# The root of the mean square in a decoder kernel: multiplied in by GpSimd behind the gating, from a product in four 32-column tiles

## The reference

```python
gg = (x @ Wg.T).reshape(B, L, H, DH)
o = o * jax.lax.rsqrt(jnp.mean(o * o, -1, keepdims=True) + EPS)
o = o * o_norm_w * jax.nn.silu(gg)
return (o.reshape(B, L, KEY_DIM) @ Wo.T, final_state)
```

## Time and profile before

| | |
|---|---|
| median of 3 timed runs | 1228.74 us (1227.93 to 1232.73) |
| profiled execution, its own time | 1221.33 us |
| its span | 1219.5 us |
| TensorE busy | 1145.7 us, 94% |
| TensorE weight loads | 790.1 us, 65% |
| VectorE busy | 814.1 us, 67% |
| ScalarE busy | 716.0 us, 59% |
| GpSimd busy | 499.3 us, 41% |

### The profile page before, as it was taken

One profiled execution on the slowest core, in us unless ns is written; L12 is line 12 of the kernel. 1 busy time (PEld: TensorE's weight loads), 2 busy tenths in 40 slices (PEclk: granted clock), 3 DMA queues, 4 the chain that ended last, 5 costly groups with the idle time before them and its releaser, 6 DMA issues.

```text
span 1219.5 us, 30002 instructions
## 1 busy us (share of the span) xinstructions
PE 1145.7 (94%) x12192; PEld 790.1 (65%) x12192; DVE 814.1 (67%) x1454; ACT 716.0 (59%) x1212; POOL 499.3 (41%) x709
## 2 busy tenths in 40 slices
PE   7888899999999999999998989859999999999987
PEld 2444455555555555555555556649998998998976
DVE  4897667768768768668576665665665566655552
ACT  3776467677677676776775866624444434445433
POOL 1659576575675774773774811100011000001000
PEclk9999799999999999999998999989999999999999
DMA  3123222323323223243326422161111122111100
GB/s 118 46 52 79 66 52 60 107 58 72 87 58 93 68 73 77 77 128 89 91 73 150 151 62 72 47 235 45 44 45 49 50 52 70 44 44 48 30 17 10
DMA packets 134602, 88.07 MB, mean 72 GB/s; under 512 B 79264, under 2 KB 118048, under 8 KB 133568
## 3 DMA queue, kind: packets, MB, share of 16 engines
q1 hardware_dynamic: 133312, 85.93, 25.9%
q10 hardware_dynamic: 1152, 0.21, 0.1%
HBM read 54.77 MB, written 14.55 MB: 57 GB/s over the span
## 4 chain that ended last, share of the span: by engine, by line
PE 75%; POOL 8%; DVE 5%; issue 4%; ACT 3%; SPq 2%; DMA 2%; ACTq 0%; POOLq 0%; DVEq 0%
PE proj L467 20%; PE out L1494 5%; PE turned_v_chain L1494 5%; PE gram L482 4%; PE turned_v_chain L1560 4%; PE proj L1552 4%; PE proj L1433 4%; POOL inverse L1204 3%; POOL rank_one L1201 3%; PE out L491 2%; PE turned_v_chain L596 2%; PE gram L1468 2%; PE decays L497 2%; PE turned_v_chain L629 2%; DVE conv L992 2%
## 5 line engine op out<-in xcount | busy, mean ns | idle before, releaser
L992 DVE SCALAR_TENSOR_TENSOR conv<-proj,kq_weights,conv 128x504 f32<-128x504 f32 (+2 forms) x261 | 189.9, 731 | 24.4 <-ACT conv L736 17.7
L467 PE MATMUL proj<-xT,vg_weights 128*128 128x512 f32 x384 | 190.6, 620 | 1.8 <-DVE conv L992 1.6
L1791 POOL TENSOR_TENSOR rope<-rope_part,rope_part 128x512 f32<-128x512 f32 x32 | 40.0, 1271 | 364.8 <-DVE rope_part L1730 364.8
L992 DVE SCALAR_TENSOR_TENSOR conv<-proj,vg_weights,conv 128x504 f32<-128x504 f32 (+2 forms) x192 | 140.8, 734 | 44.9 <-ACT conv L736 40.0
L467 PE MATMUL proj<-xT,kq_weights 128*128 128x512 f32 x348 | 164.5, 599 | 0.2 <-DVE conv L992 0.2
L1204 POOL TENSOR_TENSOR inverse<-inverse,rank_one 128x30 f32<-128x30 f32 (+14 forms) x240 | 125.2, 522 | 18.8
L1201 POOL TENSOR_TENSOR rank_one<-inverse 128x30 f32<-128x30 f32 (+14 forms) x240 | 117.7, 490 | 15.9
L467 PEld LDWEIGHTS proj<-xT,vg_weights 128*128 128x128 f32 x384 | 68.4, 192 | 65.6 <-issue 59.8
L467 PEld LDWEIGHTS proj<-xT,kq_weights 128*128 128x128 f32 x348 | 62.4, 190 | 72.8 <-issue 70.3
L1569 ACT ACTIVATE rstd<-rstd 128x1 f32<-128x1 f32 x48 | 9.8, 203 | 142.6 <-DVE rstd L1677 142.6
L482 PEld LDWEIGHTS gram<-keys_q 128*64 128x64 f32 x896 | 57.6, 138 | 54.7 <-ACT keys_q L747 36.4
(11 more groups left out here) (244 smaller groups left out, 2464.0 us busy)
## 6 DMA issues: line engine op xcount, KB each, us to landing
kq_weights<-in_kq_w SPq DMA_DIRECT2D x32, 390.0 KB, 3.5
vg_weights<-in_vg_w SPq DMA_DIRECT2D x32, 390.0 KB, 4.0
o_scratch<-oT SPq DMA_DIRECT2D x32, 256.0 KB, 2.9
o_in<-o_scratch SPq DMA_DIRECT2D x16, 512.0 KB, 4.1
diagonal<-gram_decayed SPq DMA_DIRECT2D x128, 32.0 KB, 1.9
inverse<-inverse SPq DMA_DIRECT2D x32, 128.0 KB, 2.7
q_first<-rope SPq DMA_DIRECT2D x128, 32.0 KB, 1.9
q_second<-rope SPq DMA_DIRECT2D x128, 32.0 KB, 1.9
```

The source lines that it names most:

```text
L467: mm = e.matmul(bank(c, u)[:], w[:, (k * 3 + c % 3) * 128:(k * 3 + c % 3 + 1) * 128], xT[g][:, k, :], start=(k == 0), stop=(k == KD - 1))
L992: e.scalar_tensor_tensor(acc(c, u)[:, :, back:], src[:, :, 0:S - back], weights(c, u)[:, j:j + 1], acc(c, u)[:, :, back:], ALU.mult, ALU.a ...
L1791: e.tensor_tensor(turned[half][:].rearrange("p b r q -> p r b q"), parts[2 * half][:], parts[2 * half + 1][:], op).then_inc(s_turned, 1)
```

## The change

Units 0 to 21 (`by_rows`) get a new path; units 22 to 31, whose norm falls into the drain, keep the 128x128 product and the full 128x512 Ln and Exp.

- The product: four matmuls with 32 of the 128 columns of `ones_mean`, one for each 128 tokens; matmul j writes the 32 partitions from 32j on, columns 0 to 127 of VB. So partition 32j holds the means of the j-th quarter of the tokens.
- Ln and Exp work on 128x128 (`rs4`).
- SyncE, at the head of its slot, issues four DMAs that spread row 32j of `rs4` to all 128 partitions of the j-th quarter of `o_rs`. The stores of the KRS kind move from the end of their slot to behind these, in the next slot.
- For all units VectorE now gates with silu(G) alone and waits for neither Ln nor Exp; it does so as soon as OB and the gate are there. GpSimd multiplies `oT` by `o_rs` in place, behind the first part of its elimination (`s_gr`), in the drain too, where VectorE's `scale_gate` goes. SyncE's store waits for that.

```diff
+        by_rows = lambda u: u < U - LAG - 1
@@ sync
                 for s in range(SLOTS):
+                    if live(uo) and by_rows(uo):
+                        e.wait_ge(s_rs, uo + 1)
+                        wait(e, s_gr, uo)
+                        for j in range(4):
+                            e.dma_start(o_rs[:, j * TILE:(j + 1) * TILE],
+                                        rs4[RB * j:RB * j + 1, None, :].broadcast_to([1, 128, TILE])).then_inc(d_rs, 16)
+                    rotated = prepare_at(s - 1)
+                    if rotated is not None and rotated[1] == KRS:
+                        prepare_store(*rotated)
...
                     if live(uo):
-                        e.wait_ge(s_og, uo + 1)
+                        e.wait_ge(s_gr, uo + 1)
                         e.dma_start(o_scratch[:, 4 * group(uo):4 * group(uo) + 4, head(uo), :],
...
-                    if now is not None:
+                    if now is not None and now[1] != KRS:
                         prepare_store(*now)
@@ tensor
                 def norm(u):
                     e.wait_ge(s_osum, u + 1)
-                    e.matmul(VB, ones_mean[:], o_sum[:], start=True, stop=True).then_inc(s_norm, 1)
+                    if by_rows(u):
+                        for j in range(4):
+                            mm = e.matmul(VB[rows(j), 0:TILE], ones_mean[:, 0:RB], o_sum[:, j * TILE:(j + 1) * TILE],
+                                          start=True, stop=True)
+                    else:
+                        mm = e.matmul(VB, ones_mean[:], o_sum[:], start=True, stop=True)
+                    mm.then_inc(s_norm, 1)
@@ scalar
                 def silu_gate(u):
-                    wait(e, s_gr, u - 2)
+                    wait(e, s_og, u - 2)
...
-                        wait(e, s_og, uo)
-                        e.activation(o_rs[:], VB, ACT.Ln, scale=float(2 ** O_SHIFT), bias=guard[:, 0:1]).then_inc(s_ln, 1)
+                        if by_rows(uo):
+                            wait(e, d_rs, 64 * uo)
+                            o_ln, o_mean = rs4[:], VB[:, 0:TILE]
+                        else:
+                            e.wait_ge(s_gr, uo)
+                            o_ln, o_mean = o_rs[:], VB
+                        e.activation(o_ln, o_mean, ACT.Ln, scale=float(2 ** O_SHIFT), bias=guard[:, 0:1]).then_inc(s_ln, 1)
...
-                        e.activation(o_rs[:], o_rs[:], ACT.Exp, scale=-0.5).then_inc(s_rs, 1)
+                        e.activation(o_ln, o_ln, ACT.Exp, scale=-0.5).then_inc(s_rs, 1)
@@ vector
-                def scale_gate(u):
-                    e.wait_ge(s_rs, u + 1)
-                    e.wait_ge(s_silu[G], u + 1)
-                    wait(e, s_og, u)
-                    e.tensor_tensor(o_rs[:], flat(gate[u % 3]), o_rs[:], ALU.mult).then_inc(s_gr, 1)
...
                     def gate_output():
-                        if s > U:
-                            scale_gate(uo)
-                        e.wait_ge(s_gr, uo + 1)
+                        e.wait_ge(s_osq, uo + 1)
+                        e.wait_ge(s_silu[G], uo + 1)
...
-                        e.scalar_tensor_tensor(oT[uo % 2][:], OB[:], onorm[:, 0:1], o_rs[:], ALU.mult,
+                        e.scalar_tensor_tensor(oT[uo % 2][:], OB[:], onorm[:, 0:1], flat(gate[uo % 3]), ALU.mult,
                                                ALU.mult).then_inc(s_og, 1)
@@ gpsimd
-                    if live(uo) and s <= U:
-                        e.wait_ge(s_rs, uo + 1)
-                        e.wait_ge(s_silu[G], uo + 1)
-                        wait(e, s_og, uo)
-                        e.tensor_tensor(o_rs[:], flat(gate[uo % 3]), o_rs[:], ALU.mult).then_inc(s_gr, 1)
...
                     elif solving:
                         eliminate(h, CUTS[cut][0])
                         if cut == 3:
                             scale_columns()
+                    if live(uo):
+                        e.wait_ge(s_og, uo + 1)
+                        if by_rows(uo):
+                            e.wait_ge(d_rs, 64 * (uo + 1))
+                        else:
+                            e.wait_ge(s_rs, uo + 1)
+                        e.tensor_tensor(oT[uo % 2][:], oT[uo % 2][:], o_rs[:], ALU.mult).then_inc(s_gr, 1)
@@ token tiles, vector
+                        if u3 == 0:
+                            e.wait_ge(done["scaled"], U)
                         if live(u3):
                             sums(1, u3)
```

More of the change, by code:

```diff
@@ L194, in delta_phase @@
         gate = [t(f"gate{i}", [128, GB, S]) for i in range(3)]
-        o_sum, o_rs = t("o_sum", [128, GT]), t("o_rs", [128, GT])
+        o_sum, o_rs, rs4 = t("o_sum", [128, GT]), t("o_rs", [128, GT]), t("o_rs_quarters", [128, TILE])
         n2, inv, rho, kln, kn = (t(n, [128, RB]) for n in ("n2", "inv", "rho", "k_ln", "k_norm_turned"))
@@ L230, in delta_phase @@
             "d_w_ab", "d_small", "d_ident", "d_const", "d_late", "d_diag", "d_inverse"))
+        d_rs = sem("d_o_rs")
         d_x = [sem(f"d_x{i}") for i in range(NG)]
@@ L1318, in delta_phase @@
     tiles["ints"], tiles["scales"] = ints, scales
-    done = {"o": s_og, "stored": d_out, "weights": d_w, "first": d_first, "uvo": d_uvo, "ffn": s_wgt, "ints": d_ints, "decays": s_ee,
+    done = {"o": s_og, "scaled": s_gr, "stored": d_out, "weights": d_w, "first": d_first, "uvo": d_uvo, "ffn": s_wgt, "ints": d_ints, "decays": s_ee,
             "gram": s_gm, "gate": s_silu[G], "v1": s_conv[V1], "high": s_wlo, "low": s_wloout, "solve": s_solve}
@@ L1507, in loop @@
                             if u4 == 0:
-                                e.wait_ge(done["o"], U)
+                                e.wait_ge(done["scaled"], U)
                                 e.wait_ge(done["ffn"], 2 * KD + 1)
```

## The result

| | before | after |
|---|---|---|
| median of the timed runs | 1229.82 us (1227.93 to 1232.73, 4 runs) | 1210.22 us (1208.36 to 1210.77, 4 runs) |
| profiled execution: time, span, granted clock | 1221.33, 1219.5, 0.986 | 1210.69, 1208.9, 0.982 |

The ratio of the times is 0.9836, 95% interval 0.9812 to 0.986.

A forecast was written before the change was run, and what follows sets the result against it. TensorE was taken to bound the steady stage and GpSimd's last elimination the drain up to 707 us. Terms -9.4 + 1.9 - 1.5 - 2.2 = -11.2 us gave 1217.5 us, own range 1212 to 1221, wide range 1209 to 1228.

The forecast's parts named there:

- From the profile to the median: Whole kernel: the 7.4 us between profiled execution and timed median stays the same, turning 1210.1 into 1217.5 us.
- The product over partitions: Mean-square product on TensorE, units 0 to 21: four small matmuls save 0.47 us a unit, 20 counted, 9.4 us.
- All four tiles at once: Bound chosen for the small product on TensorE: four tiles run together, 0.37 to 0.43 us, taken as 0.40.
- pairs: Rival for the small product: tiles run two at a time, saving 0.24 us a unit; 1222.1 us, chance 0.12.
- open weight loads: Rival: each small pass waits for its own weights, product 2.0 us; 1249.5 us in all, chance 0.06.
- SyncE's queue: Four 64 KB broadcasts at the slot's start take 2.62 us to issue, land in 2.3 us, rows there near 412.7.
- Cover in full: SyncE's queue costs nothing, unless GpSimd's multiplication comes later than about 3 us before the slot's end.
- sign of failure: The forecast fails if diagonal copies land late behind the output's store, or idle time shows in the steady stage.
- GpSimd in the steady stage: The moved 1.27 us multiplication fits in 2.31 us of idle time before the addition; no term.
- The drain, GpSimd part: Last batch's elimination: two multiplications add 2.5 us, starting 0.7 us earlier; net +1.9 us, between +0.5 and +4.4.
- The drain, TensorE part: After 707 us, three waits of output products for VectorE's gating, 0.3 to 0.7 us each, go: -1.5 us.
- The last unit: Gating no longer waits for Ln and Exp, so TensorE's 2.17 us wait before the next stage goes: -2.2 us.

The follow-up runs named there:

- before, repeated: The kernel before the change, unedited, timed and profiled again: 1226.96 us over 10 runs, ratio 1.0; profiled span 1226.7 us.
- after, 1st repetition: The changed kernel, unedited, timed again beside the kernel before: 1213.24 us over 6 runs, ratio 0.990.
- after, 2nd repetition: The changed kernel, unedited, timed once more as the measure for two later variants: 1215.12 us over 6 runs, ratio 0.9901.
- the order alone: Changed kernel with the old full product for all units and no broadcasts, keeping the new order of gating, multiplication and stores: 1224.93 us, ratio 0.9994.
- addition first: Changed kernel, with GpSimd's addition of query squares before its multiplication in slots where no elimination precedes the multiplication: 1212.54 us, ratio 0.9887.

## Why the prediction was right, and where it was off

**The sum.** It said -11.2 us. The profiled executions differ by 10.6 us, the two repetitions by 11.3 and 9.9. Of the 62 executions of before and 16 of after whose clock is listed the medians are 1226.2 and 1212.1, 14.2 apart, and the lines through time against clock stand 13.8 apart at 0.981. The direction and the main mechanism held; the size is between 10 and 14. The first comparison's 19.6 lies above that, and its 1210.22 us lie under the forecast's own range (1212 to 1221) though within the wide one (1209 to 1228). (By its own terms the own range is 1214 to 1220, and the chance 0.76 is 0.75.) So what bears out the -11.2 is the profiles and the repetitions, and there too the single terms agree less well than their sum. The profiled executions stage by stage, as differences to the profiled execution of before (us; starts of the products of units 0 and 21, of the turn behind the last elimination, of the last product and of the turn of x, then the end):

| stage | term of the sum | before, repeated | after | after, 1st repetition | after, 2nd repetition |
|---|---|---|---|---|---|
| to unit 0 (fill) | none | +0.5 | +1.1 | +1.4 | +1.8 |
| unit 0 to 21 | -9.4 | +0.3 | -8.95 | -7.2 | -8.0 |
| to the turn | +1.9 | +0.3 | -1.6 | -0.2 | +1.2 |
| to the last product | -1.5 | +1.5 | -0.2 | +3.5 | +3.3 |
| to the turn of x | -2.2 | +0.9 | +0.4 | -2.2 | -2.2 |
| to the end | none | +3.6 | -1.35 | -1.5 | -1.4 |
| sum | -11.2 | +7.2 | -10.6 | -6.2 | -5.3 |

The fill and the end had no term, and each differs by 1 us or more in all three executions of after; why is not known. That the whole came within 1 us in the first profile is in part luck.

**From the profile to the median: this step failed.** The 7.4 us between before's profiled execution and its median were carried over as if they belonged to the kernel. Some 4.9 of them belonged to that execution, one of the nine at the highest clock seen (0.986): it lies so far under the median of all 62. The other 2.5 belonged to the three timed runs, whose median is above that of the 62. After's profiled execution lies 0.5 us above its median. Without this step the forecast would have been 1210.1 us from the profile, and 1215 as 1226.2 - 11.2 from the pooled median.

**The product over partitions.** All four tiles at once was right, pairs (0.24 us a unit) and open weight loads fell: eight loads lie in the 0.16 us of the first row of after. The term was undersized: 0.36 us and not 0.40 for the product, and the saving 2.78 - 1.91 - 0.36 = 0.51 us, 0.04 more. The Trainium skill, TensorE: Matmul & The Clock Gate, Part 3, lets weight loads overlap matmuls in flight only when row groups differ; here all rows are shared and this trace does not agree with it, as its 128*64 rows did not before.

**SyncE's queue: the landing was mis-sized.** 2.3 us assumed, bounds 1.9 and 2.7; 6.2 us measured. Both bounds came from copies whose sources were many partitions, and nothing in them was a bound for one partition read 128 times. "Cover in full" then held in 17 slots of 21, where the elimination stands ahead of the multiplication, and failed in four: 21 x 0.51 = 10.7 us, less the 2.2 of these slots, and 0.46 more at unit 19 by the chance of a load, became 8.95. The prediction had named this case ("about one where no elimination precedes it") and priced it at nothing. Its own sign of failure, idle time in the steady stage, did show, if only for 1.9 us in all. Instead of 20 x 0.47 = 9.4: too small a saving, too many good slots, nearly the same sum.

**GpSimd in the steady stage.** The addition of the longest slots still came in time; TensorE waits for GpSimd only in the four.

**The drain, GpSimd part: too dear, and its sign open.** It said +1.9 us (0.5 to 4.4), as both multiplications would lengthen the elimination. In the profile of after the turn comes 1.56 us earlier still than the 7.90 us by which unit 21 is early (-8.95, and +1.05 in the fill): -9.46. The repetitions have -0.2 and +1.2 in this stage (the table above), and the kernel with the order alone, whose drain is the same, has +1.6. Two multiplications did fall inside the elimination, but it takes only 0.3 us longer (46.5 us, and again 46.5 in one repetition; 49.2 in the other). GpSimd's groups of instructions within the elimination (count, busy us, mean ns, idle before), of before, then of after:

```profile
L1204 POOL TENSOR_TENSOR inverse<-inverse,rank_one 128x30 f32<-128x30 f32 (+14 forms) x30 | 16.2, 540 | 2.4
L1201 POOL TENSOR_TENSOR rank_one<-inverse 128x30 f32<-128x30 f32 (+14 forms) x30 | 15.6, 521 | 2.1
L1265 POOL TENSOR_TENSOR W_scaled<-W,k_norm 128x512 f32<-128x512 f32 x3 | 3.1, 1043 | 2.4 <-ACT W L838 2.4
```

```profile
L1219 POOL TENSOR_TENSOR inverse<-inverse,rank_one 128x30 f32<-128x30 f32 (+14 forms) x30 | 15.9, 530 | 2.3
L1216 POOL TENSOR_TENSOR rank_one<-inverse 128x30 f32<-128x30 f32 (+14 forms) x30 | 14.9, 496 | 2.0
L1275 POOL TENSOR_TENSOR W_scaled<-W,k_norm 128x512 f32<-128x512 f32 x3 | 3.1, 1045 | 1.5 <-ACT W L855 1.5
L1318 POOL TENSOR_TENSOR oT<-oT,o_rs 128x512 f32<-128x512 f32 x2 | 2.6, 1277 | 0.0
```

Of the 2.6 us, 0.9 fill idle time (2.4 to 1.5), and the 60 small instructions take 1.0 us less; why these are faster stays open. In the repetition with 49.2 us the same idle time, a wait for ScalarE's `W`, is 4.1 us. The elimination starts earlier against unit 21 by 2.0, 0.5 and 2.0 us in the three executions; 0.7 was counted for VectorE's multiplication, and what makes the rest is open. So the step that failed here is that the two multiplications add their full length.

**The drain, TensorE part.** The three waits for the gating after 707 are gone, as said, but 0.5 us of issue and of a wait for ScalarE is left in their place: 1.0 us of waiting went, not 1.5. The time between the turn and the last product did not follow: 82.1 us in before, and 81.9, 85.6 and 85.4 in the three executions of after, at a granted clock of 1.00, then 0.97, 0.94 and 0.94. The term had no place for the clock. A wait for value weights (2.47 us at 672.55) took the place of idle time at the turn (3.30 to 1.59), which costs nothing as long as the elimination sets the end.

**The last unit: right in size where the clock allows it.** The second repetition of after, the timeline:

```profile
788.10 1.13 PE L645 MATMUL turned_v_chain<-o_sum,ones_mean 128*128 128x512 f32 x2 [1.41 <-DVE o_sum L1080]
...
792.24 0.44 PE L1459 MATMUL turned_v_chain<-ident,x 128*128 128x128 f32 x2
```

792.24 - 788.10 = 4.14 us against 6.32: 2.2 us less, as counted, and 4.13 us in the other repetition. In the first profile of after the lower clock in this place hid it.

## What to carry to other kernels

Price a copy by a row with the same source layout, and let a broadcast read as many partitions as hold the value (the landing fell from 6.2 to 2.6 us; a gain in the total is not shown). Where an engine's queue has two steps, put the one that the bound engine waits for ahead of the one that waits for a DMA. Before adding a difference between a profile and a median to a forecast, look at the clock of the profiled execution: here the scatter that goes with the clock, 12 us in all, is as large as the gain of the change.

## What the runs showed of the hardware

**One source partition.** With four copies issued one behind another, 64 KB within SBUF land in 6.2 us from one partition, in 2.6 us from 32 or from 128 (medians), and 390 KB of weights queued behind take 6.4 instead of 3.5 us. The Trainium skill, SBUF — State Buffer, section Door 1: The DMA port swizzle, says that DMA bandwidth depends on how many of the 16 ports the partitions reach; one partition reaches one of them, 32 neighbours eight. The runs agree with it in direction from one partition to 32; between 32 and 128 they show no difference. They don't separate ports from partitions, nor either from 128 reads of the same 512 bytes.

**The lower clock behind a wait.** The granted clock is below 1.00 in stretches of the drain where TensorE has stood, and where it falls differs between executions of one kernel. The stretches 700 to 710 and 780 to 790 us of the first profile of after:

```profile
700.00:710.00 10.00, 9.75 (x182) 6.70 (x182) 7.00 (x11) 8.64 (x13) 2.33 (x2) 1.00 0.56 122
...
780.00:790.00 10.00, 9.01 (x90) 6.93 (x91) 6.88 (x11) 3.92 (x9) 1.27 (x1) 0.69 1.01 356
```

and of its second repetition, with its turn (the last row) in the timeline:

```profile
700.00:710.00 10.00, 7.34 (x69) 4.28 (x70) 5.59 (x6) 3.19 (x4) 2.56 (x3) 0.59 0.50 100
...
780.00:790.00 10.00, 6.17 (x79) 4.30 (x79) 5.31 (x10) 7.21 (x10) 1.61 (x2) 1.00 0.39 79
...
702.66 1.92 PE L607 MATMUL turned_v_chain<-kq_decayed,inverse 64*32 64x64 f32 x32 [4.01 <-DVE kq_decayed L1085]
```

After 4.01 us of idle time the same 32 matmuls take 1.92 us (1.2 GHz in part), after 1.59 us they take 1.08, as they did in before after 3.30. Yet in other executions 2.84 us of idle time (addition first) was followed by 1.82. The order alone took 1.17 after 2.88 us. So the length of the wait alone doesn't settle it in these runs. An earlier end of TensorE's work can be paid back in clock, as in the stage from the turn to the last product above, and the single drain or last unit of one trace is no measure of what an edit there is worth.
